# Norm 0 and mix 0 rearranged, with the edges gathered as records of three

## The chip, the cores and the metric

One core of a Trainium2 chip. The metric is the device time of one execution in microseconds. The kernel before takes 2364.84 us (median of 3 runs, 2361.81 to 2371.7).

## The reference

Two layers over 3125 nodes of 256 features and 100000 edges sorted by receiver (`dst`), each edge with a sender (`src`) and a weight:

```python
xn = _layernorm(x, axis=-1)
x = x + L0_gnn(xn, src, dst, ...) + L0_mix(xn[None], ...)[0]
x = x + L0_ffn(_layernorm(x)[None], ...)[0]
xn = _layernorm(x, axis=-1)
x = x + L1_gnn(xn, edge_index, edge_weight, ...) + L1_mix(xn[None], ...)[0]
x = x + L1_ffn(_layernorm(x)[None], ...)[0]
```

Only the first line pair matters here. `L0_gnn` sums the normed rows of the senders into each receiver (`segment_sum(node_feats[src], dst)`) and sends the sum through two dense layers. `L0_mix` is a linear attention with 4 heads of 32:

```python
xn = rmsnorm(x, g_pre);  q, k, v = split(xn @ w_qkv)
q = softmax(q, over the 32 of a head) * SCALE;  k = softmax(k, over all nodes and 4 memory rows)
context = einsum('bhdn,bhen->bhde', k, v);  out = einsum('bhde,bhdn->bhen', context, q)
return rmsnorm(out @ w_out + b_out, g_out) + x
```

Since q is a softmax in each of 4 heads, its 128 values of a node sum to 4 before SCALE.

## The kernel before, in words

The nodes are 25 tiles of 128 rows (`T`), in 7 groups of 4 (`G`, the last has one). Each engine runs a program written out by hand in a fixed order (`sp_program`, `act_program`, `pool_program`, `dve_program`, `pe_program`, L2191 on); semaphores are the only link, so what stands behind a waiting instruction waits too.

**Windows.** The edges are cut in 1564 windows, one for each pair of receivers, in 13 groups of 128 (`WG`), one window to a partition. `windows_dve` (L240) makes four memsets, waits for the constants and the 784 first receivers of the rows of 128 edges, and counts in 13 instructions how many are below each window's first receiver (L253). `windows_pool` (L271) gathers the row found for each window (13 indirect DMAs, L274); `begins_dve` (L259, called in group 5 of the norm) counts again inside the row and gives the window's first edge; `windows_pool` then gathers 128 receivers, 128 senders and 128 weights from there, 39 indirect DMAs (L279). `places_dve` (L304) subtracts the window's receiver from each edge's and masks what lies outside; `inside` counts the rest, and the total must be 100000 (`good`). `senders_dve` (L315) splits the sender's number in two parts of 7 bits. PE turns these tables (`keys_pe`), ACT and DVE write them as bf16 pairs (`lo2`, `key2`). `degrees_pool` (L282) sums the weights of each receiver on POOL: compare, multiply and fold, four rounds. The weights are turned and split in three bf16 parts (`parts_pe`, `highs_act`, `parts_of_dve`, L386).

**Norm and products** (`first_norm_*`, L576 to L663). For each group: DVE's statistics, ACT's root, DVE's reciprocal, ACT's normed tiles XN (L631), PE's transposes (L479), copies to XT by ACT and DVE (L485, L490), then q, k, v of each tile on PE (L662, L663) into four banks, which ACT empties with the row's scale (L645) from group 3 on.

**Mix** (`mix0_*`). `mix0_dve` (L773): subtract the maximum of q in each head, maximum of k over tiles (L763), X + XN (L771), q's sums and quotients (L752 to L756), k minus its maximum, ACT's exponentials between; then the context, masked to its heads (L812) and multiplied with w_out (`cwo`). The **loop** over groups (PE: L684 on): PE turns q (L690), ACT copies it, PE adds a one-row product of ones and the bias (L702) and the product with `cwo` (L703) in banks 2 to 5; ACT squares and sums (L733), takes the root (L736); DVE scales with `r2` and `gout0` (L827) and adds to X (L832, `xmix`).

**Counting** (`count_*`, from L1036). For each of 196 batches of 8 windows DVE writes one-hot matrices (`hots_dve`, L872), PE multiplies them into counts and weights, ACT empties the banks; the block of 16 octets before it is multiplied with the normed rows (`sums_pe`). DVE's front work there: XT times (1 + eps) (L1073), the weight parts, and the low parts of XN (L1084). What follows the counting (dense layers, experts, second layer) is not touched.

Of the kernel before, what the change touches and what calls it, by code (L numbers as in the profile page):

```python
# [16 lines left out]
T = 25  # L17
# [8 lines left out]
WG = 13  # L26
WN = WG * 128
# [43 lines left out]
def program(nc, ctx, a, out):  # L71
# [39 lines left out]
    w2c = CB[:, 553:553 + WG]  # L111
# [64 lines left out]
    high2, mid2, low2 = keys(WB, 6400), keys(r1_all, 2048), keys(r1_all, 0)  # L176
# [63 lines left out]
    def windows_dve(e, c):  # L240
# [7 lines left out]
        c.add(e.tensor_scalar(slot16, iota[:, 0:2 * T], 1.0, None, ALU.add))  # L248
        e.wait_ge(S("first"), 16)
        c.add(e.tensor_copy(firstf, firsts))  # L250
        c.wait()
        for g in range(WG):
            c.add(e.tensor_scalar(below[:, g, :], firstf, w2c[:, g:g + 1], None, ALU.is_lt, ALU.add, accum_out=cnt4[:, g:g + 1]))  # L253
        c.wait()
        c.add(e.tensor_scalar(row4, cnt4, 1.0, 0.0, ALU.subtract, ALU.max))
        c.wait()
        e.tensor_copy(row4i, row4).then_inc(S("rows"), 1)

    def begins_dve(e, c):  # L259
        e.wait_ge(S("drow"), 16 * WG)  # L260
        for g in range(WG):
            c.add(e.tensor_scalar(rowf[:, g, :], rowi[:, g, :], w2c[:, g:g + 1], None, ALU.is_lt, ALU.add, accum_out=beg4[:, g:g + 1]))
# [4 lines left out]

    def by_group(v):
        return v.rearrange("p (g n) -> p g n", g=WG)

    def windows_pool(e):  # L271
# [5 lines left out]
        for name, to, flat in (("edst", edst, a["dst"]), ("esrc", esrc, a["src"]), ("eew", eew, a["ew"])):  # L277
            for g in range(WG):
                e.indirect_dma_start(by_group(to)[:, g, :], None, flat.rearrange("(r k) -> r k", k=1),  # L279
                                     bass.IndirectOffsetOnAxis(ap=beg4i[:, g:g + 1], axis=0)).then_inc(S(name), 16)  # L280

    def degrees_pool(e):  # L282
        e.wait_ge(S("inside"), 1)
        e.wait_ge(S("eew"), 16 * WG)
        p = Chain(e, S("fold"))
        for g0, g1 in HALVES:
            prod = wprod[:, 0:g1 - g0, :]
            for r in range(2):
                p.wait()
                p.add(e.tensor_scalar(prod, by_group(wrel)[:, g0:g1, :], float(r), None, ALU.is_equal))  # L290
                p.wait()
                p.add(e.tensor_tensor(prod, prod, by_group(eew)[:, g0:g1, :], ALU.mult))
# [10 lines left out]

    def places_dve(e, c):  # L304
        e.wait_ge(S("edst"), 16 * WG)
        for g in range(WG):
            c.add(e.tensor_scalar(by_group(wrel)[:, g, :], by_group(edst)[:, g, :], w2c[:, g:g + 1], None, ALU.subtract))
        c.wait()
        c.add(e.tensor_scalar(wok, wrel, 0.0, None, ALU.is_ge))
        c.wait()  # L310
        c.add(e.scalar_tensor_tensor(wok, wrel, 2.0, wok, ALU.is_lt, ALU.mult))
        c.wait()
        e.tensor_reduce(inside, wok, AX, ALU.add).then_inc(S("inside"), 1)

    def senders_dve(e, c):  # L315
        e.wait_ge(S("esrc"), 16 * WG)
# [8 lines left out]
        e.scalar_tensor_tensor(wkey, whii, 1.0, wok, ALU.add, ALU.mult).then_inc(S("wkey"), 1)  # L325
# [13 lines left out]
    def turn_keys_pe(e, v, f):  # L339
# [2062 lines left out]
```

## Time and profile before

| | before |
|---|---|
| median of 3 runs | 2364.84 us |
| profiled execution | 2373.65 us |
| its span | 2372.2 us |
| busy PE / DVE / ACT / POOL | 2132.7 / 1727.7 / 1207.8 / 463.1 us |
| mean granted clock of PE | 0.926 |

The busy time of an engine is the sum of its instructions; PE's ends are modelled, so that pipelined products look longer than their distance. The granted clock is 1.00 at 2.4 GHz and 0.50 at 1.2 GHz. All times are counted from the start of the span.

### The profile page before, as it was taken

What the parts mean: (1) busy time and instruction counts of PE and PEld (TensorE: products, weight loads), DVE (VectorE), ACT (ScalarE), POOL (GpSimd) and SP (SyncE); (2) the same over time, 40 slices, a digit from 0 to 9 for tenths busy, and PEclk for the clock granted to TensorE, in tenths of its full rate; (3) what the DMA queues carried; (4) which work ended last, traced back from release to release, by engine and by line L of the source; (5) the groups of instructions that cost most, each with busy time, mean ns of one, the idle gap of its engine ahead of it and who ended that gap; (6) DMA issues with size and microseconds to landing.
All of it is one profiled execution on the core that took longest, in us unless ns stands there. A gap on an engine that the chain in (4) does not pass through costs nothing. (4 is left out here: it accounts for less than half of the span.)

```text
span 2372.2 us, 46527 instructions
## 1 busy us (share of the span) xinstructions
PE 2132.7 (90%) x17787; PEld 1964.9 (83%) x17787; DVE 1727.7 (73%) x3488; ACT 1207.8 (51%) x2817; POOL 463.1 (20%) x389
## 2 busy tenths in 40 slices
PE   4496999999964999998699999999997999999997
PEld 2355999999963999997477899989996999999996
DVE  5838878877568888886566555565556887888885
ACT  3324555555441777665551544454444325667774
POOL 2750000000005344444000000000000032444443
PEclk9756999999965999999698999999997999999998
DMA  6111333323442877777300466646652005777876
GB/s 197 51 37 51 111 87 88 110 85 99 138 146 87 230 231 232 227 227 209 86 1 24 117 194 191 177 117 191 189 160 94 19 28 178 223 227 227 227 231 167
DMA packets 237322, 338.85 MB, mean 143 GB/s; under 512 B 29721, under 2 KB 198758, under 8 KB 236966
## 3 DMA queue, kind: packets, MB, share of 16 engines
q1 hardware_dynamic: 208800, 296.14, 39.8%
q0 software_dynamic: 24848, 35.68, 8.3%
q10 hardware_dynamic: 3446, 3.97, 0.5%
q8 instruction: 146, 2.39, 0.4%
q14 instruction: 82, 0.67, 0.1%
HBM read 258.83 MB, written 76.90 MB: 142 GB/s over the span
## 5 line engine op out<-in xcount | busy, mean ns | idle before, releaser
L2164 PE MATMUL bank<-WB_r,XN_r 128*128 128x448 f32 x1400 | 399.7, 367 | 3.7 <-DVE WB_r L2123 3.7
L2123 DVE TENSOR_TENSOR WB_r<-WB,WB_r 128x448 fp32r<-128x448 f32 x350 | 214.1, 624 | 166.1 <-ACT WB_r L2116 165.9
L2116 ACT CAST WB_r<-WB 128x448 fp32r<-128x448 f32 x350 | 197.7, 568 | 222.1 <-PE bank L2164 216.6
L2164 PEld LDWEIGHTS bank<-WB_r,XN_r 128*128 128x128 f32 x1400 | 263.2, 188 | 26.8 <-DVE wb__r L2089 4.4
L1720 PE MATMUL bank<-SC_r,WB_r 128*128 128x256 f32 (+1 forms) x2064 | 256.7, 284 | 16.0 <-issue 14.0
L1720 PEld LDWEIGHTS bank<-SC_r,WB_r 128*128 128x128 f32 x2064 | 250.5, 193 | 20.4 <-issue 20.4
L917 ACT CAST WB_r<-bank 128x200 fp32r<-128x200 f32 x391 | 137.7, 352 | 200.3 <-PE bank L901 198.4
L1735 PE MATMUL bank<-R_r,H_r 128*128 128x256 f32 x1752 | 216.7, 283 | 4.8 <-DVE R_r L1631 4.8
L1735 PEld LDWEIGHTS bank<-R_r,H_r 128*128 128x128 f32 x1752 | 210.5, 190 | 5.1 <-issue 5.1
L1584 ACT ACTIVATE wb_<-bank,WB 128x256 f32<-128x256 f32 (+1 forms) x344 | 133.7, 477 | 98.0 <-issue 57.3
L1720 PE MATMUL bank<-SC_r,XN_r 128*128 128x256 f32 x1392 | 170.8, 282 | 6.2 <-issue 5.5
L1720 PEld LDWEIGHTS bank<-SC_r,XN_r 128*128 128x128 f32 x1392 | 166.2, 189 | 10.2 <-issue 10.0
L957 PE MATMUL bank<-H_r,WB_r 128*128 128x256 f32 x625 | 173.6, 308 | 0.0
L1294 POOL TENSOR_TENSOR XN_r<-XN,XN_r 128x320 fp32r<-128x320 f32 x10 | 10.3, 1029 | 804.3 <-DVE XN L1429 804.3
L2164 PE MATMUL bank<-WB_r,R_r 128*128 128x448 f32 x448 | 165.1, 368 | 0.0
L1592 ACT ACTIVATE yo<-yo,slot_p 128x256 f32<-128x256 f32 x118 | 53.7, 502 | 210.1 <-DVE yo L1670 210.1
L957 PE MATMUL bank<-XN_r,WB_r 128*128 128x256 f32 x625 | 157.2, 282 | 0.0
L1787 POOL DMA_INDIRECT SC<-xd,slot_i x128 | 136.7, 1068 | 98.3 <-PE bank L1747 49.2
L917 ACT COPY X<-bank 128x200 f32<-128x200 f32 x391 | 140.9, 360 | 0.0
L879 DVE TENSOR_TENSOR SC<-R,DR 128x1024 bf16<-128x1024 bf16 x196 | 134.0, 684 | 0.0
L1810 POOL DMA_INDIRECT out<-yo,slot_i x60 | 95.6, 1594 | 173.5 <-ACT yo L1592 162.9
L1810 POOL DMA_INDIRECT y<-yo,slot_i x58 | 93.9, 1618 | 165.7 <-ACT yo L1592 155.4
(422 smaller groups left out, 5333.9 us busy)
## 6 DMA issues: line engine op xcount, KB each, us to landing
WB<-adjw SPq DMA_DIRECT2D x350, 224.0 KB, 2.8
WB<-in_f_pack SPq DMA_DIRECT2D x127, 512.0 KB
WB<-in_f_pack SPq DMA_DIRECT2D x62, 640.0 KB
adjw<-X SPq DMA_DIRECT2D x24, 1600.0 KB, 7.5
WB<-in_f_pack SPq DMA_DIRECT2D x65, 516.0 KB
xd<-XN SPq DMA_DIRECT2D x15, 640.0 KB
y<-X SPq DMA_DIRECT2D x10, 640.0 KB, 3.3
X<-y SPq DMA_DIRECT2D x6, 640.0 KB, 7.4
```

Of the source, the lines that this page charges most:

```text
L879: e.tensor_tensor(by_two(hot_lo[s][:, 0:m, :]), row(iota16, o), along(lo2, o, 128), ALU.is_equal).then_inc(S("lo1"), 1)
L917: e.copy(to[b % 2][:, :, 8 * j:8 * j + 8].rearrange("p h (q r) -> p q h r", r=2), bank[:, :, i]).then_inc(S(name), 1)
L957: m = e.matmul(bk[:, 0:D], CNT[b % 2][:, h, :], x[:, h * D:(h + 1) * D], start=(h == 0 and x is xnh), stop=(h == T - 1 and x is xnl), skip ...
L1584: m = e.activation(st[:, q * w:(q + 1) * w], B[hp][:, q * TS:q * TS + w], gfun[L], bias=b[:, hc:hc + 1])
L1592: e.activation(ob[:, q, :], ob[:, q, :], ACT.Copy, scale=slot_p[:, 2 * i + q:2 * i + q + 1]).then_inc(S("obs"), 1)
L1720: m = e.matmul(B[hp][:, q * TS:q * TS + w], p[:, c * HID + hc * 128:c * HID + (hc + 1) * 128], x[:, c * w:(c + 1) * w], start=(c == 0 and ...
L1735: m = e.matmul(bk[:, s * D:(s + 1) * D], x[:, hc * w + s * 128:hc * w + (s + 1) * 128], p[:, hc * D:(hc + 1) * D], start=(hc == 0 and n == ...
L1787: e.indirect_dma_start(yin[i % 2][:, q * D:(q + 1) * D], None, XD, bass.IndirectOffsetOnAxis(ap=slot_i[:, 2 * i + q:2 * i + q + 1], axis=0 ...
L1810: e.indirect_dma_start((Y, out)[L], bass.IndirectOffsetOnAxis(ap=slot_i[:, 2 * i + q:2 * i + q + 1], axis=0), yob[s % 2][:, q, :], None, c ...
L2116: e.copy(split_w(m)[0], RAW[m % PR]).then_inc(S("whigh"), 1)
L2123: e.tensor_tensor(al, RAW[m % PR], ah.bitcast(F32), ALU.subtract).then_inc(S("wlow"), 1)
L2164: mm_ = e.matmul(conv_bank(k, band, c)[:, 0:PW], x[st][:, o], y, start=(st == 0 and i == 0), stop=(st == T - 1 and i == 2))
```

## The change

The three inputs of an edge are also laid in DRAM as records (receiver, sender, weight), and one gather fetches 128 records of a window, 1536 bytes, where three fetched 512 bytes each. `edst`, `esrc`, `eew` and `wrel`, `wlo` become strided views (every third element). Around it the norm and the mix are put in another order:

- ACT does 6 of the 13 counts (Sign with a running sum; the constants are moved by 0.5); the zero fills on SP wait for x; the xd stores come before the late weights.
- `begins_dve` moves from group 5 to group 3, `places_dve` to group 6 of the norm, ahead of the last copy; its masks become a square on ACT (`places_act`) and one compare with a running sum (`inside_dve`).
- X + XN goes from DVE to ACT (`x_sum_act`, scale rstd + 1). q, k, v are laid out in blocks of their own. The bias goes into `cwo`, since q sums to 4; the one-row products go. `senders_dve` comes before two of the q quotients.
- Two of the four weight parts and the first hots are made inside the loop; PE turns the weights there into banks 6 and 7.

The diff, cut to its core:

```diff
+        e.dma_start(CB[:, :], a["consts"]).then_inc(S("consts"), 16)
         e.dma_start(firsts, a["first"].partition_broadcast(128)).then_inc(S("first"), 16)
-        e.dma_start(CB[:, :], a["consts"]).then_inc(S("consts"), 16)
...
+        for g in range(COUNTED):
+            c.add(e.tensor_scalar(below[:, g, :], firstf, w2h[:, g:g + 1], None, ALU.is_lt, ALU.add, accum_out=cnt4[:, g:g + 1]))
+        c.wait()
+        c.add(e.tensor_scalar(row4[:, 0:COUNTED], cnt4[:, 0:COUNTED], 1.0, 0.0, ALU.subtract, ALU.max))
+        e.wait_ge(S("mix0_act"), M0A_PLACES)
+        c.add(e.tensor_scalar(row4[:, COUNTED:WG], cnt4[:, COUNTED:WG], 0.5, FIRSTS / 2 - 1, ALU.mult, ALU.add))
...
+    def windows_act(e):
+        e.wait_ge(S("consts"), 16)
+        e.wait_ge(S("set"), 5)
+        for g in range(COUNTED, WG):
+            e.activation(below[:, g, :], firstf, ACT.Sign, scale=-1.0, bias=w2h[:, g:g + 1],
+                         accum_out=cnt4[:, g:g + 1]).then_inc(S("mix0_act"), 1)
...
         e.wait_ge(S("begins"), 1)
-        for name, to, flat in (("edst", edst, a["dst"]), ("esrc", esrc, a["src"]), ("eew", eew, a["ew"])):
-            for g in range(WG):
-                e.indirect_dma_start(by_group(to)[:, g, :], None, flat.rearrange("(r k) -> r k", k=1),
-                                     bass.IndirectOffsetOnAxis(ap=beg4i[:, g:g + 1], axis=0)).then_inc(S(name), 16)
+        for g in range(WG):
+            e.indirect_dma_start(h_all[:, 384 * g:384 * (g + 1)].bitcast(I32), None, a["edges"].rearrange("(r k) -> r k", k=3),
+                                 bass.IndirectOffsetOnAxis(ap=beg4i[:, g:g + 1], axis=0)).then_inc(S("edges"), 16)
...
+    def places_dve(e, c):
+        e.wait_ge(S("edges"), 16 * WG)
+        for g in range(WG - 1):
+            c.add(place_dve(e, g))
+        c.wait()
+        place_dve(e, WG - 1).then_inc(S("mix0_dve"), 1)
+
+    def places_act(e):
+        e.wait_ge(S("mix0_dve"), M0V_REL + 1)
+        e.activation(wok, wrel, ACT.Square).then_inc(S("mix0_act"), 1)
+
+    def inside_dve(e):
+        e.wait_ge(S("mix0_act"), M0A_PLACES + 1)
+        e.tensor_scalar(wok, wok, 0.25, None, ALU.is_le, ALU.add, accum_out=inside).then_inc(S("inside"), 1)
...
+    def turn_weights_pe(e, f):
+        if f == 0:
+            e.wait_ge(S("edges"), 16 * WG)
+        e.wait_ge(S("key16"), f + 3)
+        turn_keys_pe(e, eew, f, 6 + f % 2).then_inc(S("keyT"), 1)
...
             if g:
                 turn_dve(e, 0, g - 1)
-            if g == G - 2:
+            if g == 3:
                 begins_dve(e, c)
+            if g == 6:
+                places_dve(e, c)
         turn_dve(e, 0, G - 1)
+        e.tensor_scalar(grow, rstd, 1.0, None, ALU.add).then_inc(S("mix0_dve"), 1)
...
         for k, t in enumerate(tiles_of(j)):
-            e.matmul(out_of(t), ones[0:1, :], bout0[0:1, :], start=(k % 2 == 0), stop=False, skip_group_check=True)
-            e.matmul(out_of(t), qt[j % 2][:, k * 128:(k + 1) * 128], cwo, start=False, stop=True,
+            if t % 2 == 0 and t >= 8:
+                e.wait_ge(S("xmix"), t // 2 - 3)
+            e.matmul(out_of(t), qt[j % 2][:, k * 128:(k + 1) * 128], cwo, start=(k % 2 == 0), stop=True,
                      skip_group_check=True).then_inc(S("ot"), 1)
...
+    def x_sum_act(e, tiles):
+
+        for t in tiles:
+            e.activation(X[:, t, :], X[:, t, :], ACT.Identity, scale=grow[:, t:t + 1], bias=nbias[:, t:t + 1]).then_inc(S("xsum"), 1)
+
     def mix0_act(e):
-        for i, (g, t0, n) in enumerate(groups):
-            e.wait_ge(S("qsub"), i + 1)
-            e.activation(g[:, :, 0:128], g[:, :, 0:128], ACT.Exp).then_inc(S("qexp"), 1)
-        for i, (g, t0, n) in enumerate(groups):
+        e.wait_ge(S("mix0_dve"), M0V_GROW + 1)
+        q_exp_act(e, 1)
+        x_sum_act(e, range(0, 6))
+        q_exp_act(e, 2)
+        x_sum_act(e, range(6, 14))
+        for i, (_, k, t0, n) in enumerate(groups):
...
+        q_sub_dve(e, c, 0)
+        inside_dve(e)
+        k_max_dve(e, c, 0)
         e.wait_ge(S("fill"), 16 * NF)
-        for g, _, _ in groups:
-            c.add(e.memset(g[:, :, 384:385], 1.0))
-        q_sub_dve(e, c, 0)
-        k_max_dve(e, c, 0)
-        for g in range(5):
-            x_sum_dve(e, c, g)
+        for section in sections:
+            c.add(e.memset(section.one(), 1.0))
+        q_norm_dve(e, c, 0)
         q_sub_dve(e, c, 1)
         k_max_dve(e, c, 1)
+        k_max_dve(e, c, 2)
...
-        places_dve(e, c)
+        c.add(e.tensor_scalar(bout0, bout0, 0.25, None, ALU.mult))
...
+        senders_dve(e, c)
         q_norm_dve(e, c, 1)
         q_norm_dve(e, c, 2)
         good_dve(e)
-        senders_dve(e, c)
...
-        e.tensor_scalar(cwo, B[1][:, 0:D], HEAD_SCALE, None, ALU.mult).then_inc(S("mix0_dve"), 1)
+
+        e.scalar_tensor_tensor(cwo, B[1][:, 0:D], HEAD_SCALE, bout0, ALU.mult, ALU.add).then_inc(S("mix0_dve"), 1)
...
+            if j + 1 in TURNED[0:2]:
+                parts_of_dve(e, c, TURNED.index(j + 1))
+            if j == 4:
+                hots_dve(e, 0)
...
         early_sp(e)
+        e.wait_ge(S("x_in1"), 32)
         zero_sp(e)
+        store_sp(e, XD, XN, "xd_out", xn_ready(e, 0))
         late_sp(e)
-        store_sp(e, XD, XN, "xd_out", xn_ready(e, 0))
```

## Rows read from the trace of the kernel before

**Rows 1.** Table by stretches: bounds, length, busy us (instructions) of the engines, PEclk, DMA.

```profile
137.00:192.00 55.00, 52.60 (x105) 25.01 (x104) 21.79 (x52) 14.35 (x59) 19.40 (x28) 0.50 0.17 48
200.00:260.00 60.00, 47.13 (x820) 44.90 (x821) 59.69 (x155) 29.86 (x110) 0.00 (x0) 0.76 0.26 75
400.00:500.00 100.00, 97.90 (x1565) 92.04 (x1562) 81.34 (x238) 54.20 (x205) 0.00 (x0) 1.00 0.32 91
```

**Rows 2.** Timeline from the start: start us, us, engine, line, operation, tiles, shapes.

```profile
7.29 5.98 ACTq L191 DMA_DIRECT2D X<-in_x  x1
...
9.21 1.03 DVE L253 TENSOR_SCALAR_CACHE_REDUCE WB<-WB,CB 128x784 bf16<-128x784 f32 x1
...
21.97 1.40 DVE L436 BATCH_NORM_STATS2 small<-X 128x6 f32<-128x256 f32 x4
```

**Rows 3.** ACT: its norm by groups up to 262 us, and a timeline row.

```profile
L631 ACT ACTIVATE XN<-X,small 128x256 f32<-128x256 f32 x25 | 13.1, 590 | 4.1 <-DVE small L595 2.5 <-issue 1.6
...
42.47 1.99 ACT L645 ACTIVATE WB<-bank,small 128x384 f32<-128x384 f32 x4
```

**Rows 4.** POOL, timeline from 10 us: the indirect gathers.

```profile
37.64 0.95 POOL L274 DMA_INDIRECT R<-in_dst,small  x1 [0.30 <-issue]
63.62 0.94 POOL L279 DMA_INDIRECT R<-in_dst,small  x1 [25.04 <-DVE small L266]
...
120.35 1.62 POOL L279 DMA_INDIRECT H<-in_ew,small  x1 [0.30 <-issue]
```

**Rows 5.** DVE, timeline from 50 us; at the end a group of the table by lines.

```profile
72.79 0.29 DVE L490 COPY XT<-bank 128x128 f32<-128x128 f32 x1 [5.87 <-PE bank L479]
...
78.86 7.08 DVE L771 TENSOR_TENSOR X<-X,XN 128x1280 f32<-128x1280 f32 x5
...
98.45 2.73 DVE L307 TENSOR_SCALAR H<-R,CB 128x128 f32<-128x128 int32 x13
...
106.01 0.28 DVE L797 COPY small<-bank 128x128 f32<-128x128 f32 x1
...
123.19 0.35 DVE L812 SCALAR_TENSOR_TENSOR small<-bank,small,CB 128x128 f32<-128x128 f32 x1
...
L763 DVE TENSOR_REDUCE small<-WB 128x128 f32<-128x1408 f32 x2 | 5.4, 2698 | 0.0
```

**Rows 6.** POOL's fold of degrees, and a later meeting of DVE and POOL (timelines).

```profile
124.82 2.48 POOL L290 TENSOR_SCALAR H<-H 128x896 f32<-128x896 f32 x1 [2.84 <-DMA H<-in_ew,small]
...
156.85 0.38 POOL L300 TENSOR_SCALAR small<-small 128x26 f32<-128x26 f32 x1
...
722.18 0.49 DVE L1432 TENSOR_TENSOR H_r<-H,CB 128x320 fp32r<-128x320 f32 x1
...
723.86 1.01 DVE L1429 TENSOR_TENSOR H<-H,CB 128x320 f32<-128x320 f32 x1
...
723.22 1.30 POOL L1294 TENSOR_TENSOR H_r<-H 128x320 fp32r<-128x320 f32 x1
```

**Rows 7.** The loop: PE's timeline, then DVE's.

```profile
130.31 1.04 PE L690 MATMUL bank<-CB,WB 128*128 128x128 f32 x8
...
133.46 0.70 PE L703 MATMUL bank<-yo,SC 128*128 128x256 f32 x2
...
147.66 1.22 PE L702 MATMUL bank<-rows,ones 1*128 1x256 f32 x2
...
148.57 1.67 DVE L827 SCALAR_TENSOR_TENSOR bank<-bank,small,rows 128x256 f32<-128x256 f32 x4
150.28 1.29 DVE L832 TENSOR_TENSOR X<-X,bank 128x512 f32<-128x512 f32 x2
...
191.83 0.42 DVE L832 TENSOR_TENSOR X<-X,bank 128x256 f32<-128x256 f32 x1
```

**Rows 8.** DVE's timeline behind the loop: weight part, first hots.

```profile
195.81 0.68 DVE L390 TENSOR_TENSOR WB<-bank,WB 128x512 f32<-128x512 f32 x1
...
198.60 0.36 DVE L878 TENSOR_TENSOR SC<-R,DR 128x400 bf16<-128x400 bf16 x1
```

More of the change, by code:

```diff
@@ L26 @@
 WG = 13
+FIRSTS = 784
 WN = WG * 128
@@ L529, in x_back, with __init__, rows_of_blocks, q @@
         return ready
-    QW = 385
-    qk_hi = R1[:, 1, 0:3 * QW]
-    QK = [WB[:, t * QW:(t + 1) * QW] if t < 22 else qk_hi[:, (t - 22) * QW:(t - 21) * QW] for t in range(T)]
-    groups = [(WB[:, 0:11 * QW].rearrange("p (t c) -> p t c", c=QW), 0, 11),
-              (WB[:, 11 * QW:22 * QW].rearrange("p (t c) -> p t c", c=QW), 11, 11),
-              (qk_hi.rearrange("p (t c) -> p t c", c=QW), 22, 3)]
+    class Group:
+        def __init__(self, wide, base, space, n):
+            self.wide, self.base, self.space, self.n = wide, base, space, n
+        def rows_of_blocks(self, k):
+            o = self.base + k * self.space
+            return self.wide[:, o:o + (128 + k) * self.n].rearrange("p (t c) -> p t c", c=128 + k)
+        def q(self):
+            return self.rows_of_blocks(0)
+        def k(self, n):
+            return self.rows_of_blocks(1)[:, 0:n, 0:128]
+        def one(self):
+            return self.rows_of_blocks(2)[:, :, 128:129]
+        def tile(self, i, k):
+            o = self.base + k * self.space + (128 + k) * i
+            return self.wide[:, o:o + 128 + (k == 2)]
+        def qkv(self, i):
+            o, s = self.base + 128 * i, self.space + i
+            return self.wide[:, o:o + 3 * s].rearrange("p (k c) -> p k c", c=s)[:, :, 0:128]
+    wide_wb = nc.alloc_sbuf_tensor_at("wide_wb", [128, 12000], F32, offset=at["WB"])
+    wide_r1 = nc.alloc_sbuf_tensor_at("wide_r1", [128, 4096], F32, offset=at["R1"])
+    sections = [Group(wide_wb, 0, 2838, 22), Group(wide_r1, 2048, 388, 3)]
+    QT = [sections[t // 22].tile(t % 22, 0) for t in range(T)]
+    KT = [sections[t // 22].tile(t % 22, 1) for t in range(T)]
+    VT = [sections[t // 22].tile(t % 22, 2) for t in range(T)]
+    groups = [(sections[0].q()[:, 0:11, :], sections[0].k(22)[:, 0:11, :], 0, 11),
+              (sections[0].q()[:, 11:22, :], sections[0].k(22)[:, 11:22, :], 11, 11),
+              (sections[1].q(), sections[1].k(3), 22, 3)]
     sd = small[:, 300:350].rearrange("p (k t) -> p k t", k=2)
     rs = small[:, 832:857]
+    grow = small[:, 325:350]
     qm, qd = small[:, 375:475], small[:, 475:575]
@@ L644, in first_products_act @@
         e.wait_ge(S("qk"), t + 1)
-        e.activation(QK[t][:, 0:384], qk_bank(t)[:, 0:384], ACT.Copy, scale=rs[:, t:t + 1]).then_inc(S("qkv"), 1)
+        e.activation(sections[t // 22].qkv(t % 22), qk_bank(t)[:, 0:384].rearrange("p (k c) -> p k c", k=3), ACT.Copy,
+                     scale=rs[:, t:t + 1]).then_inc(S("qkv"), 1)
     def first_norm_pe(e):
@@ L1052, in count_act @@
     def count_act(e):
-        highs_act(e)
-        e.wait_ge(S("degrees"), 1)
-        for g in range(5):
-            e.copy(xnh[:, fifth(g)], xn_all[:, fifth(g)]).then_inc(S("xnh"), 1)
+        highs_act(e, 2)
         for b in range(T + 4):
@@ L1060, in count_act @@
                     hots_act(e, 8 * b + i)
+                if b == 0 and 1 <= i < 6:
+                    if i == 1:
+                        e.wait_ge(S("degrees"), 1)
+                    e.copy(xnh[:, fifth(i - 1)], xn_all[:, fifth(i - 1)]).then_inc(S("xnh"), 1)
+                if (b, i) == (0, 6):
+                    highs_act(e, 3)
                 if i == 0 and 2 <= b < T + 2:
```

195 lines of the change are left out of this document (100 added, 95 removed).

## The prediction, made before the changed kernel ran

> **What bounds the kernel now.** I read the table by stretches first, then the timelines of DVE, PE, POOL and ACT up to 262 us, because every edit lies ahead of that point. The reader is to see three regimes. From 200 to 260 us DVE is busy 59.69 of 60 us: the counting stage starts out bound by DVE. From 400 to 500 us PE is busy 97.90 of 100 us at granted clock 1.00: later the stage is bound by PE. Nothing after 200 us waits for an absolute time, only for the stage ahead, so an earlier start of the counting shifts everything behind it. Between 137 and 192 us PE is busy 52.60 of 55 us, yet at granted clock 0.50, the 1.2 GHz level, and DVE has work for only 21.79 us [rows 1]. So the path up to the counting is: DVE's counts, the norm's chain, DVE without a gap from 72.79 to 123.54, then PE's loop that multiplies q with the folded context, 130.31 to 192.25, then DVE [rows 2, 3, 5, 7].
>
> The gathers that give the change its name are not on that path. All 39 are issued by POOL between 63.62 and 121.97 [rows 4], about 1.5 us apart; DVE starts the receivers at 98.45 and the senders later, and neither waits [rows 5]. Fewer gathers save POOL 26 issues, some 39 us, and earn nothing by themselves. What they allow is to move the work on places, weights and degrees.
>
> **Part by part.** Each part is given with the value I take and its two ends.
>
> Counts and head. Before, DVE makes 13 counts from 9.21, 0.95 us apart, and the statistics start at 21.97 [rows 2]. With 7 left DVE would be ready 5.7 us sooner, but it then waits for ACT's 6. ACT's queue is held by its last load issue until 7.29 + 5.98 = 13.27 [rows 2]. Its count has 784 columns; an activation of 256 takes about 0.52 (13.1 / 25, [rows 3]), so I estimate 1.0 us each, 6 us, and 1.3 for a table: 20.6. That is a gain of 1.4. If the issue is short now that the zero fills come after x, up to 5.7. At the low end nothing.
>
> Norm. `begins_dve` moves from the sixth group to the fourth. The last of 13 row gathers is issued at 37.64 [rows 4], so DVE will wait there about 1 us and then spend the 4 us of 13 small counts, with the next group's statistics queued behind it, ACT's norm behind those, and PE waiting for ACT to empty its banks. I price that stall at 3 us. Against it stands a stall that may go: ACT emptied the first qkv banks at 42.47 [rows 3], some 3 us later than its inputs' chain asks for, since DVE had gaps no wait explains. POOL's records then start about 45 and, at 1.25 us each, are issued by 62; `places_dve` asks for them at about 65, ahead of the last turn copy, which PE releases only at about 70. Its 3 us stay hidden. Head and norm together: 2.5 us gained, ends -3 and +7.
>
> DVE's middle. Out go the five sums of X and XN, 7.0 us from 78.86 (to ACT: 25 activations, 13.1 us by [rows 3], in a stretch where ACT mostly idles), and the places with their masks, 106.01 - 98.45 = 7.56 us [rows 5]. In comes one compare with a running sum over 1664 elements: the counts of 784 take 1.03 us [rows 2], so about 1.9. The strided reads, the scaled bias and `grow` I put at 0.8 (0 to 1.8). The reduce of k over tiles takes 2.70 us twice [rows 5]; closer tiles leave its number of elements as it is, so I take no gain, at best 2.3. Net 12 us gained, 11 to 15. Moving the senders ahead of two q norms changes their order, not the sum.
>
> The fold of degrees. Before, POOL's fold ran from 124.82 to 157.23, 32.4 us, under PE's loop, when DVE read PSUM and mostly idled [rows 6]. Now it can start once `inside` is there, about 76, and lies under DVE's busiest stretch, nearly all of it on the path. What they do to each other is shown elsewhere: DVE's product of 128x320 takes 0.49 us, and 1.01 when POOL's 1.30 us operation runs beside it [rows 6]; POOL's gather of 0.95 us is 1.62 beside DVE [rows 4]. So each waits for the other's instruction in progress. DVE has about 20 instructions with two SBUF operands there, and POOL's largest, the first of each of four rounds, lasts 2.48 us [rows 6]. At 0.3 us each I get 6 us lost, the row's own 0.52 for each gives 10; ends 0 and 14.
>
> The Trainium skill, page "SBUF — State Buffer", section "Who interferes with whom", says that a DVE instruction with two SBUF inputs contends with a GpSimd instruction that reads SBUF, and that the first comer holds the ports for its whole instruction. The 0.49 against 1.01 agrees [rows 6]. By that rule the loss is nearer 8 to 10 than 6, and the total gain 33 to 35 instead of 37.
>
> The loop. From the first q transposes (130.31) to the last sum of X (192.25) it takes 61.9 us [rows 7]. The one-row bias products go: 50 instructions. At the full clock a pair takes 0.63 of PE's time (0.70 shown, overlapping), at half 1.15 (147.66, shown 1.22). A group of four tiles then costs PE 4 x 1.15 + 1.0 = 5.6 us at 1.2 GHz instead of 10.1, and about 3.1 at 2.4 GHz. DVE's stage of a group is 0.4 + 1.67 + 1.29 [rows 7] plus 0.2 of added waits, 3.6 us. Six and a small one are 23 us; two rounds of weight parts of 2.79 us (195.81 to 198.60) and one of hots of 1.7 come in [rows 8], 30 us in all; ahead of them stand 7 us for the first group. That gives 37 to 38 if DVE sets the pace, and 43 if PE stays at half clock, where PE does. Which clock? It fell when PE, always busy, had alternated one-row and 128-row products for some 5 us, and stayed low [rows 1, 7]; where 128-row operands fill 97.9% it is 1.00 [rows 1]. Without the one-row products I lean to full. I take 39.5: 22.4 us gained, ends 16 and 25.
>
> The Trainium skill, "TensorE: Matmul & The Clock Gate", Part 1, ties the low clock to idleness. The row of 52.60 busy us in 55 at 0.50 [rows 1] speaks against that as a full account, and the measurement decides. By the rule alone the old loop should have run at 2.4 GHz and the new one would gain nothing by the clock; what the low level would cost the new loop is the 43 above.
>
> Front of the counting. Two of four weight parts (2.79 us each) and the first hots (1.7) are done inside the loop, 7.3 us less for DVE behind it [rows 8]; DVE has no idle time there [rows 1]. PE at half clock may take some of it back: 6, ends 3 and 7.3.
>
> SP's order: the zero fills now stand behind x, the xd stores ahead of the late weights. Fills must land before tile 22 is emptied, about 75 us, and the weights before XT is scaled, about 165; the xd stores end with the norm, near 70, in either order. Nothing, but up to 2 us if a store is late.
>
> **The sum.** 2.5 + 12 - 6 + 22.4 + 6 = 36.9 us. The profiled execution took 2373.65 us (span 2372.2), so it would be 2336.8; it is itself 8.8 above the median of 2364.84. Taken off the median: 2328.
>
> **The rivals.** (a) The lock and the low clock both bite: 14 for the fold, the loop at 43 to 45, a 3 us stall in the norm. 0 + 11 - 14 + 18 + 4 = 19: 2346. For it: both mechanisms are in the rows; against it: both at their ends together. (b) No stall in the norm, full clock, a fold that mostly falls beside reduces, which have one input, and the faster k reduce: 6 + 14 - 2 + 24 + 7 = 49: 2316. (c) The rebuild does not do what it says: the counting takes back what it is given, because at its start PE is cold and the sums of the second block are bound by PE; then only about half passes, 18 us: 2347. Against it: DVE has no wait up to 260 us. (d) Slower: the gather of 12-byte records is cut into its records. There would be 13 x 128 x 128 = 213 thousand pieces. POOL writes a gather of 128 pieces in 0.95 us, 7.4 ns a piece; even at a tenth of that the pieces cost 158 us, and as `places_dve` stands ahead of the norm's last copy all of it beyond about 25 us is on the path: about 2460 and more. It decides from about 62 us of gathering on. Against it: the old edge gathers had one-element rows, 128 to a partition, and were issued in the same 0.95 us as the 128-element ones [rows 4].
>
> **How the numbers follow.** Forecast 0.62, (a) 0.15, (b) 0.10, (c) 0.08, (d) or another loss of its kind 0.05. The terms' ends, not all at once, make 2328 into 2314 to 2343; (a), (c) and (b) reach a little over it, so I give 2313 to 2345. A measurement here tells about 0.5%, 12 us, from no change. Faster by more: 0.93 (all but (d) and a piece of (a) and (c)); within: 0.03; slower: 0.04.
>
> **What would show it.** Right: 13 record gathers ended by about 63; no DVE instruction on X + XN; DVE's masked context near 116; q transposes near 123; loop near 40 us, PE's product pairs 0.70 again; first windows right behind the loop. The fold's cost shows as q and k passes longer than 1.6 us. Wrong: DVE waiting for the record DMAs ahead of the last turn copy, a norm stage longer than before, or granted clock 0.50 all through the loop.

## The result and the profile after

The changed kernel takes 2349.70 us (median of 4 runs, 2348.34 to 2352.94), the kernel before beside it 2368.27 (4 runs, 2361.81 to 2373.6): ratio 0.9912, 95% interval [0.9892, 0.9932]. It is faster by 0.9%, 18.6 us between the medians and 23.6 between the profiled executions (2373.65 and 2350.05), where 36.9 were forecast. 2349.7 lies above the range that was given, 2313 to 2345.

Five marks cut the time in pieces: the end of DVE's copy of the norm's last turn, the end of the masked context (DVE), PE's first q transposes, the end of DVE's last sum of X in the loop, and the first pair sums of the counting (line `e.tensor_tensor(to, to, B[4 + b % 2]...)`, L980 before, L1074 after).

| us from the span's start | before | after | piece before | piece after | forecast |
|---|---|---|---|---|---|
| last turn's copy ends (norm) | 73.08 | 85.93 | 73.1 | 85.9 | 70.6 |
| masked context ends (middle) | 123.54 | 135.94 | 50.5 | 50.0 | 44.5 |
| q transposes begin | 130.31 | 142.47 | 6.8 | 6.5 | 6.8 |
| last sum of X ends (loop) | 192.25 | 177.49 | 61.9 | 35.0 | 39.5 |
| first pair sums begin (front of counting) | 246.25 | 225.21 | 54.0 | 47.7 | 48.0 |
| end of the span (rest) | 2372.2 | 2348.5 | 2125.9 | 2123.3 | 2125.9 |

The stretches after, for [rows 1]:

```profile
142.00:178.00 36.00, 20.95 (x119) 15.96 (x118) 32.07 (x72) 19.81 (x72) 0.00 (x0) 0.87 0.22 73
200.00:260.00 60.00, 55.05 (x914) 52.03 (x912) 52.64 (x153) 31.57 (x121) 0.00 (x0) 0.95 0.39 111
400.00:500.00 100.00, 97.93 (x1561) 92.14 (x1561) 83.08 (x242) 53.83 (x204) 0.00 (x0) 1.00 0.31 88
```

In the loop PE is busy 20.95 of 36 us, no longer nearly all of it, the granted clock is 0.87 instead of 0.50, and DVE is busy 32.07: the loop has changed its bound. The later counting is as it was.

The norm is where the forecast broke. DVE's timeline, for [rows 2, 5], then ACT's and PE's:

```profile
19.95 1.41 DVE L465 BATCH_NORM_STATS2 small<-X 128x6 f32<-128x256 f32 x4
...
62.24 0.69 DVE L519 COPY XT<-bank 128x512 f32<-128x512 f32 x1 [9.42 <-remote]
72.66 0.69 DVE L519 COPY XT<-bank 128x512 f32<-128x512 f32 x1 [6.04 <-PE bank L508]
73.27 2.99 DVE L325 TENSOR_SCALAR H<-H,CB 128x128 f32<-128x128 int32 x13
85.64 0.29 DVE L519 COPY XT<-bank 128x128 f32<-128x128 f32 x1 [9.38 <-PE bank L508]
```

```profile
62.18 0.58 ACT L514 COPY XT<-bank 128x512 f32<-128x512 f32 x1 [7.25 <-remote]
...
76.30 1.52 ACT L715 ACTIVATE wide_wb<-bank,small 128x384 f32<-128x384 f32 x3 [3.49 <-DVE H L325]
```

```profile
55.35 1.04 PE L508 MATMUL bank<-CB,XN 128*128 128x128 f32 x8
63.40 1.62 PE L733 MATMUL bank<-wb_,XT 128*128 128x384 f32 x2 [7.01 <-ACT wide_wb L715]
...
70.30 0.81 PE L733 MATMUL bank<-wb_,XT 128*128 128x384 f32 x2
...
77.02 1.62 PE L733 MATMUL bank<-wb_,XT 128*128 128x384 f32 x2 [4.40 <-ACT wide_wb L715]
```

The reader is to see two holes. In the first, PE has made the fifth turn's transposes by 56.4, and both copies of them begin only at 62.2. The profile calls the releaser remote, which means that it ties the signal to no instruction that ended near it. In the second, ACT can't empty a bank (76.30) before the places (L325) are done, and PE waits for ACT. After each hole PE's same two products take 1.62 us where they take 0.81: the low one of its two levels, which it leaves some 6 us later, so a hole costs more than its length.

Where the norm lost its time is read from the starts of DVE's copies, one for each turn (us):

| copy of turn | 2 | 3 | 4 | 5 | 6 | 7 |
|---|---|---|---|---|---|---|
| before | 33.29 | 40.93 | 51.70 | 58.78 | 66.29 | 72.79 |
| after | 31.26 | 38.89 | 49.34 | 62.24 | 72.66 | 85.64 |
| e1_order | 31.02 | 38.69 | 49.33 | 62.03 | 70.94 | 79.37 |
| e3_gather_later | 31.04 | 38.67 | 48.26 | 55.41 | 62.50 | 84.86 |
| e9_begins_back | 31.29 | 39.04 | 49.62 | 56.70 | 64.21 | 70.71 |
| e7_bias_back | 31.21 | 36.87 | 45.32 | 56.60 | 63.69 | 72.12 |
| e14_both_again | 31.04 | 36.36 | 45.16 | 56.44 | 63.53 | 69.96 |
| e13_parts_after | 31.35 | 36.40 | 44.30 | 51.39 | 58.89 | 65.39 |

Up to the fourth turn the changed kernel is 2.4 us ahead. It then loses 5.8 us in the fifth turn (the first hole), 2.9 in the sixth (PE at the low level behind it) and 6.5 in the seventh (the second hole).

POOL, for [rows 4, 6]: records, then the fold.

```profile
43.73 0.94 POOL L297 DMA_INDIRECT H<-in_edges,small  x1 [7.18 <-DVE small L288]
...
58.73 0.95 POOL L297 DMA_INDIRECT H<-in_edges,small  x1 [0.30 <-issue]
91.11 2.98 POOL L308 TENSOR_SCALAR H<-H 128x896 f32<-128x896 f32 x1 [31.43 <-DVE R L340]
...
138.67 0.37 POOL L318 TENSOR_SCALAR small<-small 128x26 f32<-128x26 f32 x1
```

A gather of 128 records costs 0.95 us to issue, as one of 128 words did, and the last bytes are there about 62: no sign of small pieces. The fold took 32.4 us before and takes 47.9 now (91.11 to 139.04), nearly all of it beside DVE's middle, which ends at 135.94.

### The profile page after: what moved, and what is told of

The parts are those of the page before. It is cut to its first block and busy times, and to the rows that moved or that the text cites. A ratio compares the mean times of both kernels' runs of the same rounds, so it can differ in the third digit from the quotient of the medians.

```text
span 2348.5 us, 46441 instructions
## 1 busy us (share of the span) xinstructions
PE 2094.3 (89%) x17737; PEld 1948.1 (83%) x17737; DVE 1723.9 (73%) x3473; ACT 1227.1 (52%) x2856; POOL 442.9 (19%) x363
## 3 DMA queue, kind: packets, MB, share of 16 engines
q8 instruction: 145, 2.38, 0.4%
## 5 line engine op out<-in xcount | busy, mean ns | idle before, releaser
L1680 ACT ACTIVATE wb_<-bank,WB 128x256 f32<-128x256 f32 (+1 forms) x344 | 133.6, 476 | 99.0 <-issue 63.5
L1816 PEld LDWEIGHTS bank<-SC_r,XN_r 128*128 128x128 f32 x1392 | 166.6, 189 | 10.6 <-issue 10.5
L1390 POOL TENSOR_TENSOR XN_r<-XN,XN_r 128x320 fp32r<-128x320 f32 x10 | 10.3, 1028 | 803.8 <-DVE XN L1525 803.8
L1883 POOL DMA_INDIRECT SC<-xd,slot_i x128 | 136.7, 1068 | 97.1 <-PE bank L1843 47.6
```

Of the source, the lines that this page charges most:

```text
L1680: m = e.activation(st[:, q * w:(q + 1) * w], B[hp][:, q * TS:q * TS + w], gfun[L], bias=b[:, hc:hc + 1])
L1816: m = e.matmul(B[hp][:, q * TS:q * TS + w], p[:, c * HID + hc * 128:c * HID + (hc + 1) * 128], x[:, c * w:(c + 1) * w], start=(c == 0 and ...
L1883: e.indirect_dma_start(yin[i % 2][:, q * D:(q + 1) * D], None, XD, bass.IndirectOffsetOnAxis(ap=slot_i[:, 2 * i + q:2 * i + q + 1], axis=0 ...
```

## The experiments

Fourteen runs in four batches, each batch on one chip with the kernel before beside it. In the table the pieces are those of the marks above, from one profiled execution each; the ratio is to the kernel before of the same batch.

| run | norm | middle | loop | front | first pair sums | median | ratio [95%] |
|---|---|---|---|---|---|---|---|
| e1_order | 79.7 | 49.9 | 35.0 | 47.8 | 218.96 | 2344.17 | 0.9878 [0.9848, 0.9909] |
| e2_fold_late | 85.8 | 40.4 | 41.3 | 47.7 | 221.66 | 2347.13 | 0.9893 [0.9863, 0.9923] |
| e3_gather_later | 85.2 | 50.0 | 35.0 | 47.6 | 224.30 | 2350.28 | 0.9895 [0.986, 0.993] |
| e4_before_bias | 72.6 | 50.7 | 31.0 | 54.0 | 214.13 | 2341.12 | 0.9865 [0.9835, 0.9894] |
| e5_places_late | 71.3 | 50.7 | 35.5 | 48.4 | 212.41 | 2337.81 | 0.9888 [0.986, 0.9916] |
| e6_both | 69.8 | 44.1 | 40.8 | 48.3 | 209.64 | 2333.36 | 0.9874 [0.9845, 0.9904] |
| e7_bias_back | 72.4 | 50.0 | 62.0 | 48.0 | 238.92 | 2363.05 | 0.9981 [0.9954, 1.0009] |
| e8_records | 67.7 | 61.1 | 62.1 | 54.0 | 251.51 | 2379.80 | 1.0047 [1.0026, 1.0067] |
| e9_begins_back | 71.0 | 44.1 | 40.9 | 48.4 | 211.15 | 2337.54 | 0.9866 [0.9836, 0.9897] |
| e10_records_fold | 73.1 | 52.7 | 63.5 | 54.0 | 249.69 | 2379.36 | 1.0038 [1.0013, 1.0063] |
| e11_bias_again | 72.6 | 50.7 | 29.1 | 54.0 | 213.21 | 2340.47 | 0.9874 [0.9835, 0.9912] |
| e12_after_again | 85.4 | 50.1 | 35.0 | 47.8 | 224.83 | 2352.80 | 0.9928 [0.9906, 0.9951] |
| e13_parts_after | 65.7 | 44.1 | 31.3 | 55.5 | 203.77 | 2332.66 | 0.985 [0.9837, 0.9864] |
| e14_both_again | 70.3 | 44.3 | 40.8 | 48.4 | 210.33 | 2336.06 | 0.9863 [0.9848, 0.9878] |

The pieces repeat within 0.3 us from chip to chip, but for the norm and one loop (31.0 and 29.1). The rest behind the first pair sums lies between 2118.5 and 2127.7 us without a pattern that follows an edit. So a verdict on a mechanism is read from its piece, and the ratios only from differences over 0.3%.

**e1_order: the numbers of the places and lengths exchanged.** ACT's emptying of tile 12 and later waits for `M0V_RS2 + 1` counts of one semaphore. In the changed kernel that number stands behind the places', though DVE computes the lengths before the places.

```diff
-        0, 2, 3, 4, 5, 6, 7, 8, 12, 13, 14, 15)
+        0, 2, 4, 3, 5, 6, 7, 8, 12, 13, 14, 15)
```

> The changed kernel with two numbers of one semaphore exchanged: ACT may empty tiles 12 to 24 as soon as the second set of row scales is there, and no longer waits for the places as well. Theory A (ACT's wait for the places held PE 4.40 us, and PE came back at half clock): DVE's last turn copy falls from 85.6 to about 80, the time by 5 to 6 us against the changed kernel, ratio to the kernel before 0.989. Rival (the wait is hidden; PE would have waited for the copies to XT anyway): copy at 84 to 86, ratio 0.991 to 0.992. In both the idle stretch of all engines from 56 to 62 us stays.

The copy ends at 79.66 instead of 85.93, and everything behind it is as long as in the changed kernel. Not all of the 6.3 us are the edit's: the sixth turn's copy is 1.7 us earlier already, and the wait for tile 12 stands behind that copy. There PE came back from the first hole sooner, at 0.81 again by 66.64 instead of 69.65. From the sixth to the seventh copy it is 8.43 us instead of 12.98: 4.6 us were a number in a list, not work. Kernels with the places elsewhere need less still, 6.43 (e14) to 6.50 (before): the places and their square on ACT, which e1 still has there, cost 2.0.

**e2_fold_late: the fold waits for `cwo`.**

```diff
         e.wait_ge(S("edges"), 16 * WG)
+        e.wait_ge(S("mix0_dve"), M0V_CWO + 1)
```

> The changed kernel with POOL's fold of the degrees held back until DVE has written cwo (about 138 us less what is won), so that it lies under the loop as before. Theory B (POOL's fold and DVE's two-operand instructions block each other): DVE's stretch from the last turn copy to the masked context falls from 50.0 us to 38 to 40, the time by 10 to 12 us against the changed kernel, ratio about 0.987; the fold itself falls from 47.6 to about 33 us. Rival (DVE's passes are long for another reason, the strided views or the new layout of q, k, v): the stretch stays at 46 to 50 and the three products of the senders stay over 2 us each, ratio 0.991. Degrees are then ready at about 160, before ACT asks for them at 175.

The middle is 40.4 us instead of 50.0: the fold beside it costs 9.6. Three instructions of the senders, first in the changed kernel, then here:

```profile
119.28 4.22 DVE L348 SCALAR_TENSOR_TENSOR H<-DR,H 128x1664 f32<-128x1664 f32 x1
123.54 3.05 DVE L350 SCALAR_TENSOR_TENSOR DR<-DR,H 128x1664 f32<-128x1664 f32 x1
126.62 2.17 DVE L352 SCALAR_TENSOR_TENSOR R<-DR,R 128x1664 f32<-128x1664 f32 x1
```

```profile
113.74 2.48 DVE L349 SCALAR_TENSOR_TENSOR H<-DR,H 128x1664 f32<-128x1664 f32 x1
116.25 2.48 DVE L351 SCALAR_TENSOR_TENSOR DR<-DR,H 128x1664 f32<-128x1664 f32 x1
118.76 1.89 DVE L353 SCALAR_TENSOR_TENSOR R<-DR,R 128x1664 f32<-128x1664 f32 x1
```

The wait for the other engine is inside the duration of the instruction, so no gap shows it. In the loop, though, the fold now costs 6.3 us (41.3 for 35.0), which the forecast did not have: it took the loop for a place where DVE reads PSUM.

**e3_gather_later: the records behind the fifth turn's copy** (on top of e1).

```diff
         e.wait_ge(S("begins"), 1)
+        e.wait_ge(S("xt1"), 5)
```

> As e1_order, and POOL issues the 13 record gathers only when the fifth copy to XT by DVE is done, so that they don't run from 43.7 to 61. Theory C (the stretch from 56 to 62 in which all engines stand still is made by the record gathers in flight): the fifth copy starts at about 56.5 instead of 62.2 and PE has no 7 us gap there; the gathers then end at about 75 and the places wait for them, with the last copy behind them (about 79), so the end is near e1_order or some us better or worse. Rival (it belongs to this place of the program, as a fetch of instructions that takes its time): the gap of 6 us stays at the fifth copy, or reappears a few instructions on, with no gather in flight; then the time is 10 us above e1_order.

The first hole is gone: the fifth turn's copy is at 55.41 instead of 62.03 (e1) and the sixth's at 62.50 instead of 70.94. But the places ahead of the last turn wait 12.3 us for the records and begin at 75.50. Theory C holds for the hole, and the total is no better because the places stand where they do.

**e5_places_late** (on top of e3) moves them: behind the first maximum over K, with the square on ACT first in the mix.

```diff
-            if g == 6:
-                places_dve(e, c)
...
         k_max_dve(e, c, 0)
+        places_dve(e, c)
```

> The kernel after the change with three orders altered: the record gathers wait until the copy of the fifth turn (as in the run with later gathers), the emptying of the q|k|v tiles waits for nothing but its lengths, and the places stand behind the first maximum over K instead of ahead of the last turn. Theory A (the norm lost its time to the places and to the gathers beside it): the last turn's copy ends at 66 to 69 us instead of 85.9, the middle grows by the 3.0 us of the places to about 53, unless the lock weighs more; the loop stays 35. Time about 12 us under the changed kernel: ratio to the kernel before 0.984 to 0.987. Rival B (the standstill belongs to the place in the norm, not to the gathers): the copy ends at 73 or later and the ratio is 0.987 to 0.989. Rival C (the edges land too late for the places, as in the run with later gathers, 75.4 us): the middle begins earlier but stands still for over 3 us, and half of the gain is lost.

The norm is 71.3, not 66 to 69; the middle 50.7 with the places in it. The first pair sums are 6.6 us earlier than in e1, but e1 ran on another chip. On e5's own chip stands e7, with the norm and the middle of e1: there the masked context ends at 122.41, in e5 at 122.00. So up to there the new order itself is worth 0.4 us, and the rest comes with the chip (below, e12). **e6_both** adds the late fold:

> The same with the fold also behind the head weights, as in the run with the late fold. Theory A (the lock costs about 10 us in the middle and about 6 in the loop, measured in that run): about 3.5 us faster than its neighbour without the late fold: ratio 0.982 to 0.985, and at or under the kernel before without its bias products (0.9865 on the first chip). Rival: with the middle ending at about 110 us, the fold (32 to 48 us) ends behind the loop, and the copies of XN that wait for the degrees are late: no faster than its neighbour.

Middle 44.1 for 50.7, loop 40.8 for 35.5: 1.3 us in these two pieces, 4.5 between medians. Both pairs with and without the late fold (e2, e6) thus show the same exchange: 9.6 and 6.6 won in the middle, 6.3 and 5.3 given back in the loop.

**e4_before_bias: the kernel before with one edit,** the bias in `cwo` instead of one-row products.

```diff
-            e.matmul(out_of(t), ones[0:1, :], bout0[0:1, :], start=(k % 2 == 0), stop=False, skip_group_check=True)
-            e.matmul(out_of(t), qt[j % 2][:, k * 128:(k + 1) * 128], cwo, start=False, stop=True,
+            e.matmul(out_of(t), qt[j % 2][:, k * 128:(k + 1) * 128], cwo, start=(k % 2 == 0), stop=True,
```

> The kernel before with one thing of the change: the one-row bias products are gone, the bias is in cwo. Theory D (the loop's gain is this edit's, by fewer products and by the clock): the loop from the first q transposes to the last sum of X takes about 40 us instead of 61.9 if the granted clock stays at 1.00, ratio 0.990 to 0.991. Rival (the clock falls to 0.50 all the same, since PE idled before): 44 to 48 us, ratio 0.993 to 0.994.

The loop is 31.0 us, below the 40 expected, and this single edit (2341.12) beats the whole change. **e11_bias_again** is the same kernel beside e9 and e12:

> The kernel before without its one-row bias products, again, to stand on the same chip beside the others. All theories: ratio 0.984 to 0.989, loop 31 us; the fast combination is under it by 2 to 8 us if the rest of the change is worth anything.

It is 12 us under the changed kernel on the same chip (2340.47 against 2352.80, and no run of the one reaches into those of the other). **e7_bias_back** is the other side: e1 with the products back.

> The changed kernel with the corrected order of its numbers, and with the 25 one-row bias products back in the loop. Theory A (the one-row products are nearly the whole of the loop's gain): the loop is 60 to 66 us instead of 35, PE's granted clock in it 0.5 to 0.6, and the time is within 0.5% of the kernel before (ratio 0.997 to 1.003 less the 7 us of the corrected order). Rival B (the sums of X on ACT and the finer steps gave half of it): the loop is 45 to 52, ratio about 0.993.

Loop 62.0 us, as before the change (61.9), though X + XN is on ACT and the steps are finer. The whole 27 us of the loop's gain are the one-row products. Its loop and the part of it behind 153 us, then PE's timeline where the clock falls:

```profile
129.00:191.00 62.00, 59.64 (x166) 31.25 (x163) 31.80 (x70) 20.12 (x72) 0.00 (x0) 0.57 0.13 43
...
153.00:191.00 38.00, 35.87 (x96) 18.24 (x94) 17.57 (x44) 10.39 (x43) 0.00 (x0) 0.50 0.16 52
```

```profile
134.62 1.07 PE L779 MATMUL bank<-yo,SC 128*128 128x256 f32 x2
...
137.33 1.22 PE L778 MATMUL bank<-rows,ones 1*128 1x256 f32 x2
...
149.59 0.69 PE L778 MATMUL bank<-rows,ones 1*128 1x256 f32 x2
150.21 0.70 PE L779 MATMUL bank<-yo,SC 128*128 128x256 f32 x2
...
152.25 1.22 PE L778 MATMUL bank<-rows,ones 1*128 1x256 f32 x2
153.40 1.22 PE L779 MATMUL bank<-yo,SC 128*128 128x256 f32 x2
```

PE fell to 1.2 GHz twice, near 135 and at 152, both times without a gap; between them, from 148 to 152, it was at 2.4 GHz, and no run shows why. From the second fall it stayed low to the end of the loop, busy 35.87 of 38 us. In the four loops with one-row products (before, e7, e8, e10) the mean granted clock is 0.53 to 0.57, in the twelve without them 0.78 to 0.90.

**e8_records: the kernel before with nothing but the records,** what the title of the change says.

```diff
-        for name, to, flat in (("edst", edst, a["dst"]), ("esrc", esrc, a["src"]), ("eew", eew, a["ew"])):
-            for g in range(WG):
+        for g in range(WG):
+            e.indirect_dma_start(h_all[:, 384 * g:384 * (g + 1)].bitcast(I32), None, a["edges"].rearrange("(r k) -> r k", k=3),
```

> The kernel before with nothing but the records: 13 gathers of 12-byte records instead of 39 of 4-byte ones, and the views with a stride of three words. Theory A (nothing waited for the gathers but the fold): ratio 0.998 to 1.002; the gathers end at about 80 us instead of 122, the last turn's copy stays at 73, the fold starts at 112 instead of 125 and lies over more of the middle, which takes 1 to 3 us longer. Rival B (the strided views cost DVE time, 4 us): slower, ratio 1.002 to 1.004. Rival C (the early fold ends earlier and frees the loop from the lock): ratio 0.996 to 0.998.

Slower, ratio 1.0047 [1.0026, 1.0067]. The last weights no longer hold the fold back: POOL begins it at 101.69 instead of 124.82, in the middle, which takes 61.1 us instead of 50.5.

```profile
101.69 2.89 POOL L288 TENSOR_SCALAR H<-H 128x896 f32<-128x896 f32 x1 [25.88 <-DVE small L311]
```

```profile
101.82 4.24 DVE L799 TENSOR_TENSOR WB<-WB,small 128x1408 f32<-128x1408 f32 x2
105.98 2.57 DVE L799 TENSOR_TENSOR R<-R,small 128x256 f32<-128x256 f32 x1
```

In the kernel before, without the fold beside them, the same two rows (L801) took 3.16 and 0.42 us.

**e10_records_fold** holds the fold back behind `cwo` by the same line as e2.

> The records alone in the kernel before, and the fold behind the head weights. Theory A (what made the records alone slower was the fold, which then began 23 us earlier and lay over the middle, 61.1 us instead of 50.5): the middle is 50 to 52 again, the loop stays 62 (PE sets it), ratio 0.997 to 1.001. Rival B (the strided views themselves cost the 10 us): the middle stays 58 or more and the ratio 1.004. Each for the same start of the norm.

The middle is 52.7: 8.4 of the 10.6 us were the fold, the other 2.2 are the strided views. The places make 0.9 of them (13 subtractions 2.86 for 2.73 us, the masks 1.27 for 1.03 and 2.37 for 1.89), the senders 1.4 (1.28, 2.48 and 2.38 us for 1.00, 1.89 and 1.89). Yet the ratio, 1.0038, hardly moved. Its loop is 1.6 us longer (63.5), and its first pair sums are 3.4 us later than in the kernel before; between the medians lie 8.8 us. The rest of this stays open.

**e12_after_again** asks whom the first hole belongs to.

> The changed kernel itself once more, for its norm. Theory A (the standstill of all engines at 56 to 62 us belongs to this kernel's gathers): the fifth turn's copy is at 62 again with 9 us of wait ahead of it, ratio 0.991. Rival B (it belongs to a chip or an execution: the run with the bias products back had the same gathers and none): no wait on a remote releaser over 1 us between 35 and 62 us, the fifth turn's copy at about 56.6, last copy at 78 to 80 (the number order still costs 6), ratio 0.989 to 0.991.

The hole is there again, 10.32 us of wait. With the gathers at the same time, the fifth turn's copy in e12, then in e7:

```profile
62.44 0.69 DVE L519 COPY XT<-bank 128x512 f32<-128x512 f32 x1 [10.32 <-remote]
```

```profile
56.60 0.69 DVE L519 COPY XT<-bank 128x512 f32<-128x512 f32 x1 [6.24 <-PE bank L508]
```

So neither theory is whole. The hole comes with the gathers at 43 to 60 us (e3 and e9 on the same chips, with later gathers, have none) and, it seems, only on certain chips, though no single kernel was profiled on both kinds: all profiles of the batch with e5 to e8 and of that with e13 and e14 lack also the remote wait of 1.4 to 2.4 us ahead of the third turn's copy near 40, which all the others have, the kernel before too. In all four profiles with the hole (the changed kernel, e1, e2, e12) ACT's copy begins 0.2 to 0.4 us behind the gather queue's last packet (between 61.6 and 62.0). Why a signal from PE should wait for them no run here shows.

**e9_begins_back**: e6 with the begins at their old turn, the gathers straight behind them, the places behind the third q group.

```diff
-            if g == 3:
+            if g == G - 2:
                 begins_dve(e, c)
```

> The changed kernel with the corrected order of numbers and the late fold, the begins back at the turn where the kernel before has them (so that the record gathers follow at about 62 to 78 us) and the places behind the subtraction of the third Q group. Theory A (the begins beside the fourth turn hold up the norm, and places and inside are as cheap elsewhere): the last turn's copy ends at 64 to 67 us instead of 69.8 of the run with both, the middle stays 44, the loop 41, and the time is 3 to 5 us under that run: ratio 0.983 to 0.986, the fastest of all. Rival B (the begins cost the same wherever they are): ratio as the run with both, 0.987. Rival C (the edges land behind the places' turn): the middle stands still for some us, ratio 0.988 or more.

The norm is 71.0, no shorter than in e6, but on the chip with the remote wait; so this run does not decide. Its successor **e13_parts_after** has the same norm on the other kind of chip: 65.7, against 70.3 of **e14_both_again** (e6 again) beside it. On that kind of chip the begins at the fourth turn cost 4.6 us. On the other kind nothing of it is seen: e3, with the begins there, has its sixth turn's copy at 62.50, e9, without, at 64.21. e13 also takes the first two weight parts and the first hots out of the loop.

```diff
-            if j + 1 in TURNED[0:2]:
-                parts_of_dve(e, c, TURNED.index(j + 1))
-            if j == 4:
-                hots_dve(e, 0)
```

> The run with the begins back, with the first two parts of the weights and the first pair's one-hot rows moved from the loop to just behind it, and the last two turns of the weights behind the loop on PE. Theory A (the lock stretches what the change moved into the loop): in the loop with the fold beside it the two parts took 9.4 us where they took 5.6 without the fold, and the loop 40.9 where the kernel before without bias products, also with the fold beside it, took 31.0. With them behind the loop the loop is 31 to 34, the way from its end to the first pair sums 53 to 55 instead of 48.4, and the sum of both 3 to 5 us shorter: ratio 0.983 to 0.986, and 3 to 5 us under its neighbour. Rival B (the work is only moved and the finer steps of the loop cost the rest): the sum of both stays 88 to 90, the ratio that of its neighbour, 0.987.

> The run with both (corrected order, gathers after the fifth turn, places in the middle, late fold) again, for the same chip as its neighbour. Theory A: ratio 0.986 to 0.988; first pair sums at 209 to 213 us. It also tells whether its norm of 69.8 us was its own or the chip's: if its own, the last turn's copy ends at 69 to 70.5 again; if the chip's, at 71 to 76, with waits on a remote releaser between 35 and 39 us.

Loop and front together are 86.8 us for 89.1: Theory A in kind, but 2.3 us is less than the 3 that it asked for. The medians of e13 and e14 lie 3.4 us apart, and the norm's 4.6 would be more than all of that, so only the pieces speak for the theory. In the loop of e6, with the fold beside it, and in that of e1 without:

```profile
L914 DVE SCALAR_TENSOR_TENSOR bank<-bank,small,rows 128x256 f32<-128x256 f32 x25 | 11.1, 486 | 0.2
L423 DVE CAST R<-WB 128x1024 bf16<-128x1024 f32 x2 | 3.8, 1896 | 0.1
L425 DVE TENSOR_TENSOR WB<-WB,R 128x512 f32<-128x512 f32 x2 | 2.4, 1202 | 0.1
```

```profile
L914 DVE SCALAR_TENSOR_TENSOR bank<-bank,small,rows 128x256 f32<-128x256 f32 x25 | 11.1, 487 | 0.2
L421 DVE CAST R<-WB 128x1024 bf16<-128x1024 f32 x2 | 1.4, 694 | 0.1
L423 DVE TENSOR_TENSOR WB<-WB,R 128x512 f32<-128x512 f32 x2 | 1.4, 694 | 0.1
```

The products whose data come from PSUM take 486 and 487 ns; the cast and the difference between SBUF tiles take 2.7 and 1.7 times as long. The old loop had hardly any of the second kind, which fits its 31.0 us with most of the fold beside it (e4), though no run has that loop without the fold. e13 is the fastest of all, 2332.66 us, ratio 0.985 [0.9837, 0.9864], below the interval of the changed kernel.

## Why the prediction was wrong

The direction and most of the mechanisms held; the sum failed in the norm above all, and at the fold and in the middle by less, and gained in the loop.

- **Head: right.** The statistics begin at 19.95, 2.0 us earlier (1.4 taken).
- **Norm: the step that failed.** "Head and norm together: 2.5 us gained, ends -3 and +7" came out as -12.9. The records were issued by 59.7, as foreseen, and the places did not wait for them. Two losses stood at nothing. The first is "Its 3 us stay hidden": the places, ahead of the last copy, held ACT's emptying of tile 12 through a number of a semaphore (4.6 us, e1), which stood in the diff, and even without that they and their square on ACT cost 2.0. The second had no term at all: the hole while the gathers run, 5.8 us, and 2.9 more at the low clock behind it; e3 is 8.4 us ahead of e1 at the sixth copy. Why the hole comes stays open. The begins, priced at 3, are not among these losses: they cost 4.6 on the kind of chip of e13 and e14, and nothing seen on that of e3 and e9, whose remote waits the changed kernel's profile shows too. "A stall that may go" did not go: between the third and the fourth copy lie 10.45 us, and 10.77 before.
- **DVE's middle: right in kind, just under its low end of 11.** Without the fold 50.5 became 40.4 (e2): 10.1 of the 12 taken. The strided reads were put at 0.8; the senders alone lost 1.5 by them (1.31, 2.48 and 2.48 us in e2 for 1.00, 1.89 and 1.89 before). The reduce of k is unchanged (2.72 and 2.71 us).
- **The fold: mis-sized.** -6 was taken, -9.6 measured. By the rule of the Trainium skill ("SBUF — State Buffer", "Who interferes with whom") 8 to 10 was worked out beside it, and the 9.6 of this case agree. Over the 20 instructions that the forecast counted that is 0.48 each, near the row's 0.52 and not the 0.3 chosen, which had no row behind it. The loss is uneven: a subtraction of 0.56 us took 2.47 beside the fold (L835), one of 3.16 took 3.17 (L885).
- **The loop: right in kind, mis-sized by hedging.** Its own working, 30 us of DVE steps and 7 ahead of them, gives 37; 2.5 were added for the clock. Measured: 5.7 ahead (142.47 to 148.16) and 29.3, 35.0 in all, 26.9 gained for 22.4. DVE sets the pace at granted clock 0.87. For the rule of the Trainium skill ("TensorE: Matmul & The Clock Gate", Part 1), that the low clock comes of idleness, e7 is a counter-case: busy 35.87 of 38 us at 0.50, and once the one-row products go 0.87 at 20.95 us busy of 36. The norm's holes of 7.01 and 4.40 us, after which PE is slow, fit that rule, so idleness is one way to the low level here and not the only one. What it is about the one-row products that brings it, no run shows.
- **Front of the counting: right.** 6.3 for 6. **SP's order:** no wait for fills or weights appears.
- **The gathers "earn nothing by themselves": too kind.** By themselves they lose 0.4 to 0.5% (e8, e10). In e8 it is the fold, brought forward over busy ground; in e10, with the fold back, 2.2 us are the strided views, and most of the rest stays open.

Of the 36.9 forecast, 15.4 were lost in head and norm, 3.6 at the fold and 1.9 in the middle; 4.5 came back in the loop and 3.2 in small pieces, 2.6 of them behind the first pair sums, where the spread is larger than that: 23.7 by pieces, 23.6 measured. The rival nearest to the result by number is (c), 2347: the counting takes back what it is given. It did not; the front took 47.7 us for 48.0 and the rest behind it no longer than before. Rival (a), 2346, had the fold and a stall in the norm, but also a slow loop, which did not come. Both are near by luck.

## What to carry to other kernels

Find the edit that pays, and run it alone: here one small algebraic step (the bias folded into the matrix, since the values that multiply it sum to a constant) gave 27 to 31 us of a loop of 62 (e7, e4), and the large rebuild around it, as it stood, cost about 12 of them again (e11 and e12, one chip). When work is freed to start earlier, ask what it will run beside: moving POOL's fold from a stretch where DVE reads PSUM to one where it works between SBUF tiles cost 10 us. Where several engines count on one semaphore, check that each number is reached in the order in which the work is done.

## What the runs showed of the hardware

- What POOL's fold costs DVE is hidden in durations and shows as no gap: 4.22, 3.05 and 2.17 us for three instructions of the senders that take 2.48, 2.48 and 1.89 without it (e2), 1896 ns for a cast of 694 (e6, e1); DVE's reduces of 1.61 us and its products on PSUM (486 ns) were not touched.
- PE fell from 2.4 to 1.2 GHz without a gap where one-row and 128-row products alternated, pairs of 0.70 us becoming 1.22; the mean granted clock of that loop was 0.53 to 0.57 with the one-row products and 0.78 to 0.90 without.
- Views with a stride of three words made DVE's instructions of 1664 elements longer: 2.48 us for 1.89, 1.28 for 1.00, 1.27 for 1.03 (e10 and the kernel before).
- A gather of 128 records of 12 bytes per partition is issued in 0.95 us like one of words or of rows of 512 bytes; the instruction that waits for the last of them began 2.6 us behind the last issue (e3, 72.9 to 75.5).
- Waits on a remote releaser in the norm, 1.4 to 2.4 us near 40 in ten profiles and 9.2 to 10.3 near 62 in four of them, are absent in all six profiles of two other chips.
